# Splat attention and a mixture-of-experts layer: the second half of the heads prepared inside the head loop

## What is computed

```
xn = layernorm(x)
q, k, v = heads of xn @ Wq.T, Wk.T, Wv.T               # 16 heads of 16
feats(z) = exp(-0.5*|z-pos|^2/scale^2), tanh((z-pos).dir)   # 8 splats a head
splat    = (amp*qg) @ kg.T + strength*(amp*qg*qd) @ (kg*kd).T
std = softmax(causal(q k.T/4)) v ; gsa = softmax(causal(q k.T/4 + sens*splat)) v
attn = ((1-blend)*std + blend*gsa) @ Wo.T
idx, w = top 2 of 16 by sqrt(softplus(xn @ gate_w.T)) + gate_b
y = sum of w * expert(xn) over the rows' slots (at most 128 rows an expert)
shared = (silu(xn @ Ws1.T) * (xn @ Ws3.T)) @ Ws2.T
out = x + attn + y + shared
```

## Time and profile before

| | us |
|---|---|
| median of 3 runs | 377.26 (376.95 to 378.29) |
| the profiled execution | 378.75 |
| its span, first to last instruction | 376.9 |

### The profile page before, as it was taken

The page is one execution under the profiler, slowest core; times in us unless marked ns, Lnnn a source line. Parts: engine busy times, 40 slices in busy tenths (PEclk is TensorE's granted clock), DMA queues, the critical chain, the costliest instruction groups (busy, mean ns, idle before and its releaser), DMA issues.

```text
span 376.9 us, 6181 instructions
## 1 busy us (share of the span) xinstructions
PE 334.7 (89%) x2172; PEld 174.8 (46%) x2172; DVE 230.7 (61%) x614; ACT 194.1 (51%) x278; POOL 65.7 (17%) x82
## 2 busy tenths in 40 slices
PE   0999996788979999999999999999999999989965
PEld 0643663343345544554455445544554454335433
DVE  4555857587674665567556655766577558776222
ACT  1699824525414365436543654366346547767530
POOL 7200140400047530110111011102010007710000
PEclk9999768598979999999999999999999999999995
DMA  6408623304341354245655565547555525510011
GB/s 220 131 0 103 107 38 41 60 13 60 47 135 15 41 75 73 71 89 102 142 153 105 113 139 153 107 93 154 129 125 111 79 53 127 143 42 2 0 57 56
DMA packets 27330, 33.01 MB, mean 88 GB/s; under 512 B 6593, under 2 KB 20097, under 8 KB 27297
## 3 DMA queue, kind: packets, MB, share of 16 engines
q1 hardware_dynamic: 23745, 28.32, 37.4%
q0 software_dynamic: 2128, 4.22, 3.9%
q10 hardware_dynamic: 1424, 0.04, 0.2%
HBM read 15.60 MB, written 4.28 MB: 53 GB/s over the span
## 4 chain that ended last, share of the span: by engine, by line
PE 72%; DVE 14%; ACT 9%; issue 3%; DMA 1%; SPq 0%; DVEq 0%; ACTq 0%
PE ps L817 16%; PE ps L745 9%; PE ps L800 8%; PE ps L788 7%; PE ps L754 7%; PE ps L718 6%; ACT arena_p L636 6%; DVE mx L1093 5%; PE ps L676 4%; PE ps L773 2%; PE ps L695 2%; PE ps L758 2%; PE ps L791 2%; DMA acc<-in_x_dram 1%; ACT small L641 1%
## 5 line engine op out<-in xcount | busy, mean ns | idle before, releaser
L636 ACT ACTIVATE arena_p<-ps 128x1024 f32<-128x1024 f32 (+1 forms) x192 | 147.2, 811 | 79.4 <-PE ps L800 53.7
L1093 DVE TENSOR_REDUCE mx<-ps 128x1 f32<-128x512 f32 (+3 forms) x160 | 89.3, 590 | 33.2 <-PE ps L718 22.7
L817 PE MATMUL ps<-arena_p,v_full 128*32 128x512 f32 (+3 forms) x768 | 72.6, 496 | 0.6 <-ACT arena_p L636 0.6
L718 PE MATMUL ps<-stage 96*128 96x512 bf16 (+3 forms) x160 | 51.5, 362 | 7.1 <-DVE mx L1093 4.7
L788 PE MATMUL ps<-stage 98*128 98x512 bf16 (+1 forms) x192 | 51.9, 337 | 4.7 <-ACT arena_p L636 4.2
L800 PE MATMUL ps<-stage 98*128 98x512 bf16 (+1 forms) x192 | 47.4, 332 | 3.0 <-ACT arena_p L636 2.4
L641 ACT ACTIVATE small<-ps 128x176 f32<-128x176 f32 x24 | 7.6, 318 | 64.1 <-PE ps L745 64.1
L387 POOL DMA_INDIRECT wt<-xn_scratch,ids_sb x16 | 15.2, 951 | 133.2 <-PE ps L735 127.6
L817 PEld LDWEIGHTS ps<-arena_p,v_full 128*32 128x32 f32 x768 | 20.2, 110 | 35.4 <-issue 30.3
L754 PE MATMUL ps<-arena_o,small 88*128 88x256 f32 x96 | 27.4, 409 | 8.3 <-DVE small L1116 6.3
L788 PEld LDWEIGHTS ps<-stage 98*128 98x128 bf16 x192 | 18.8, 100 | 23.5 <-ACT arena_p L636 9.8
(11 more groups left out here) (193 smaller groups left out, 418.5 us busy)
## 6 DMA issues: line engine op xcount, KB each, us to landing
w_sb<-in_w_dram SPq DMA_DIRECT2D x16, 352.0 KB
stage<-split SPq DMA_DIRECT2D x48, 96.0 KB, 2.9
stage<-split SPq DMA_DIRECT2D x48, 64.0 KB, 2.7
arena_o<-in_w_dram SPq DMA_DIRECT2D x16, 176.0 KB
stage<-split SPq DMA_DIRECT2D x80, 32.0 KB, 2.5
ye_scratch<-wt SPq DMA_DIRECT2D x16, 128.0 KB, 1.8
stage<-split SPq DMA_DIRECT2D x32, 48.0 KB
acc<-in_x_dram SPq DMA_DIRECT2D x2, 512.0 KB, 4.6
```

The costliest lines, as they stand in the source:

```text
L636: A(to, ps[:, 1 + 2 * s:3 + 2 * s, off:CH], ACT.Exp, scale=SCALE).then_inc(done, 1)
L718: ins = M(b[:, 0:n1 - n0], lhs, ks[0:KR, pr, h, n0:n1], start=True, stop=not diag)
L817: ins = M(ps[c:c + 2 * HD, 0, off:CH], v_full[:, jb + s, g * GH + h, :], of, start=jb + s == 0, stop=end)
L1093: V.reduce_max(mx[:, it // TC, h, it % TC, pc:pc + 1], b[:, 0:n1 - n0], AX.X).then_inc(aux_free, 1)
```

## The change

The heads are prepared in two halves. Before the loop only heads 0 to 7 get projections, features and parts; the second half's are tasks in the table: projections (`proj1`) at slots 26 to 31 counted over all groups (24 a group), features (`feat1`) at 34 to 39, and the parts, rests and thirds at 30 to 53, emptied by ScalarE between the exponentials; the thirds of all parts are VectorE's, and GpSimd has none. q and k features of one half now lie in the two partition halves of one tile, and a group's features are 17 transfers instead of 19. The rows of group 0 are loaded part by part, each as soon as its part is there.

Routing moves to slots 10 to 36, so its first five steps stay in group 0. All of `max1` for group 0 moves into slots 0 to 5 with its shift at 6. The experts run one after the other, every fifth slot from 52 on; the shared expert takes the place of a seventeenth, its eight tiles behind them from slot 133 to 173, and the additions start at 156. In the prologue the gate comes before the features and the values before the first maxima. The parameters arrive in one transfer, and their square root and exponentials come before the evictions.

```diff
-        PRO += [("proj", (s, m, tc)) for m in range(KD) for s in range(2) for tc in range(NC)] + [("par", 0)]
-        PRO += [("feat", (s, tc, w)) for s in range(2) for tc in range(NC) for w in range(2)]
-        PRO += [("gate", 0)] + [("v", n) for n in range(NT // 2)]
+        PRO += [("proj", (s, tc)) for s in range(2) for tc in range(NC)] + [("par", m) for m in range(2)] + [("gate", 0)]
+        PRO += [("feat", (tc, w)) for tc in range(NC) for w in range(2)] + [("v", n) for n in range(NT // 2)]
...
-        LATER = 8
-        first_rest = [(n // 2, ("pre", t)) for n, t in enumerate(max1[LATER:])] + [(4, ("pre", ("shift", 1)))]
-        first_maxima = spread_late(max0, 5, 9) + [(12, ("shift", 0))] + spread_late(max1, 10, 20) + [(22, ("shift", 1))]
+        def chain(kinds, count, at):
+            return [(at + 5 * n + step, (kind, n)) for n in range(count) for kind, step in zip(kinds, (0, 2, 4, 5))]
+        first_rest = [(n // 3, ("pre", t)) for n, t in enumerate(max1)] + [(6, ("pre", ("shift", 1)))]
+        first_maxima = spread_late(max0, 7, 11) + [(13, ("shift", 0))] + spread_late(max1, 11, 21) + [(22, ("shift", 1))]
+        HALF = [(26, ("proj1", (0, 0))), (27, ("proj1", (0, 1))), (30, ("proj1", (1, 0))), (31, ("proj1", (1, 1))),
+                (30, ("p0", 4)), (34, ("p0", 5)),
+                (34, ("feat1", (0, 0))), (35, ("feat1", (0, 1))), (38, ("feat1", (1, 0))), (39, ("feat1", (1, 1))),
+                (41, ("product", 1)), (42, ("p0", 6)), (43, ("p0", 7)),
+                (42, ("rest", 4)), (43, ("rest", 5)), (44, ("p1", 4)), (45, ("p1", 5)), (46, ("third", 4)), (47, ("third", 5)),
+                (48, ("rest", 6)), (49, ("rest", 7)), (50, ("p1", 6)), (51, ("p1", 7)), (52, ("third", 6)), (53, ("third", 7))]
+        S_ROUTE, S_EXPERT, S_SHARED, S_ADD = (10, 36), 52, 133, 156
+        long = HALF + spread([("route", k) for k in range(ROUTE)], *S_ROUTE)
+        long += chain(("xT", "gu", "hT", "y"), E, S_EXPERT)
+        long += [(at, t) for at, t in chain(("-", "sgu", "shT", "sy"), NT, S_SHARED) if t[0] != "-"]
+        long += spread([("add", (k, n)) for n in range(NT) for k in range(2)], S_ADD, 7 * NSLOT + 12)
...
-        PRE1 = max1[0:LATER]
...
+            for j in range(N_F - 1):
+                if ROWS_F[j][0:3] in ((0, 0, 0), (0, 1, 0), (0, 2, 0)):
+                    for at in (2, 3):
+                        wait_parts(sp, at, ROWS_F[j][1])
+                load_feature_row(sp, 0, 0, j, f_in[0])
+            shift_rows(-1, 0, 0)
+            sp.wait_ge(zeros_out, 16)
+            sp.wait_ge(gaps_ready, 1)
+            load_feature_row(sp, 0, 0, N_F - 1, f_in[0])
             for j in range(N_QK):
                 load_qk_row(sp, 1, 1, j, qk_in[1])
...
-                        elif (kind, a) == ("route", ROUTE - 1):
+                        elif (kind, a) == FIRST_WEIGHTS:
                             sp.wait_ge(slots_ready, 2)
-                            for e in range(WB - 1):
+                            sp.wait_ge(aux_full, full_of(("feat1", (1, 1))))
+                            for e in range(WB):
                                 expert_in(e)
...
+                            elif kind in HALVES:
+                                bank, count, _ = place(g, (kind, a))
+                                act.wait_ge(aux_full, count)
+                                if (kind, a) == ("proj1", (0, 0)):
+                                    act.wait_ge(xn_out, 16)
+                                (from_proj if kind == "proj1" else from_feat)(1, *a, ps[:, bank, :], half_free)
+                            elif kind == "p0":
+                                part0(a)
+                            elif kind == "p1":
+                                part1(a)
...
+            rest_of(0)
+            gate()
+            third_of(0)
+            rest_of(1)
+            plus_one()
+            third_of(1)
+            product(0)
             rest_of(2)
             rest_of(3)
-            product(0)
-            rest_of(4)
-            rest_of(5)
-            third_of(4)
-            product(1)
-            rest_of(6)
-            third_of(5)
-            rest_of(7)
+            third_of(2)
+            third_of(3)
```

More of the change, by code:

```diff
@@ L216, in bass_splat_attention_moe_layer @@
         max1 = [("max", (h, it, pc)) for h in range(GH) for it in range(TC, NT) for pc in range(2)]
-        def spread(tasks, first, last):
-            return [(first + (last + 1 - first) * n // len(tasks), t) for n, t in enumerate(tasks)]
         def slotted(*lists):
@@ L272, in bass_splat_attention_moe_layer @@
         PRE0 = max0 + [("shift", 0)]
-        PRE1 = max1[0:LATER]
         AB = 3
-        UNBANKED = ("add", "route")
+        FIRST_WEIGHTS = ("product", 1)
+        OWN_E = next(e for e in range(E) if AT["xT", e] >= OWN_AT[1] * NSLOT)
+        UNBANKED = ("add", "route", "p0", "p1", "rest", "third", "product")
         CUM = 4
-        sequence = [(-1, t) for t in PRE0 + PRE1]
+        sequence = [(-1, t) for t in PRE0]
         for g in range(NG):
@@ L299, in shape_of @@
             return off, jb // TC == ic
-        N_QK, N_F = 12, 19
+        ROWS_QK = [(n, 2 * n + (1 - 2 * n) * step, h) for step in range(3) for n in range(2) for h in range(GH)]
+        ROWS_F = [(n, 2 * n + (1 - 2 * n) * step, h, w) for step in range(3) for n in range(2) for h in range(GH)
+                  for w in ((0, 1) if n == 0 and step < 2 else (None,))]
+        N_QK, N_F = len(ROWS_QK), len(ROWS_F) + 1
         def load_qk_row(eng, g, b, j, done):
-            n, h = j // 6, j % 6 // 3
-            row, part, num = RUNS[j % 3]
+            n, run, h = ROWS_QK[j]
+            row, part, num = RUNS[run]
             head = g * GH + h
@@ L700, in aux @@
                 kind, a = t
[L701 removed]
+                if kind in UNBANKED and t != ("route", CUM):
                     return
[L703 removed]
+                bank, count, _ = place(g, t)
                 b = ps[:, bank, :]
                 if count > AB:
[L706 removed]
+                    pe.wait_ge(*freed[count - 1 - AB])
                 if kind == "max2":
@@ L820, in pv, with own @@
                     ins.then_inc(acc_full, 1)
-            n_v = PRO.index(("v", 0))
-            for n in range(n_v):
-                prologue(n)
-            pe.wait_ge(wide_ready, 1)
-            pe.wait_ge(pro_act, N_ACT)
-            pe.wait_ge(consts, 1)
-            needed = pe.value_load(wide[0:1, 0:1], min_val=0, max_val=1)
-            with pe.If(needed > 0):
-                pe.wait_ge(pro_dve, N_DVE)
-                with pe.Fori(0, NG) as g:
+            def own(half, b, fb):
+                with pe.Fori(half * NG // 2, (half + 1) * NG // 2) as g:
                     pe.wait_ge(own_in, (g + 1) * (16 * (N_QK + N_F - 1)))
@@ L900, in _ @@
                             slot(3)
+                if g + 1 == OWN_AT[1]:
+                    with pe.If(needed > 0):
+                        for n in range(AB):
+                            pe.wait_ge(*freed[DONE_BY[g] - 1 - n])
+                        own(1, g % QB, g % 2)
             pv(NG - 1, NP - 1)
@@ L1064, in route @@
                 elif k == CUM:
-                    bank, count = place(g, ("route", CUM))
-                    dve.wait_ge(aux_full, count)
+                    bank, full, count = place(g, ("route", CUM))
+                    dve.wait_ge(aux_full, full)
                     V.tensor_copy(G[7], ps[:, bank, 0:NT * E].rearrange("p (n e) -> p n e", e=E)).then_inc(aux_free, 1)
@@ L1083, in aux @@
                     return
-                bank, count = place(g, t)
+                if kind in HALVES or kind in ("p0", "p1"):
+                    return
+                if kind in ("rest", "third", "product"):
+                    {"rest": rest_of, "third": third_of, "product": product}[kind](a)
+                    return
+                bank, full, count = place(g, t)
                 b = ps[:, bank, :]
-                dve.wait_ge(aux_full, count)
+                dve.wait_ge(aux_full, full)
                 if kind == "max2":
@@ L1216, in _ @@
                             aux(g, t)
+                if g + 1 == OWN_AT[1]:
+                    with dve.If(needed > 0):
+                        own(1)
             evac(NG - 1, 1)
```

588 lines of the change are left out of this document (278 added, 310 removed).

## The result

The changed kernel takes **392.71 us** (median of 4 runs, 389.52 to 395.27) against 377.77 for the kernel before: a ratio of 1.0385, 95% interval 1.03 to 1.0471. The forecast was 382.5 with a range of 373 to 391, slower at 0.59. The direction was right; the time lies above the range. The profiled execution took 395.27 us, its span is 393.5, and the sum had 382.1.

What follows compares the result with a forecast made beforehand. TensorE bounds the kernel after group 0, so gains come only before 120.65 us. Sum: 97.5 + 186.7 + 46.2 + 21.0 + 12.1 + 0.6 - 1.0 + 7.0 + 12.0 = 382.1 us span; forecast median 382.5, range 373 to 391.

Steps and rivals of the forecast that it cites:

- Start of attention: Prologue to group 0's first third: first score matmul at 52.0 us, second row block's at 71.1, slot 8 at 74.1.
- half clock: Group 0, slots 0 to 7: the stall before slot 7 and sparse TensorE bring half clock, costing the sum nothing extra.
- Rest of group 0: Slots 8 to 23: 23.4 us, from VectorE's 22.7 us of work plus 0.7 for waits.
- the end of group 0 some 23 us earlier: End of group 0: at 97.5 us, where it was 120.65 before.
- routing's last step at slot 30: Routing: last step at about 108 us, scatters and gathers behind it have until slot 52 and cost nothing.
- Projections, features, parts: Second half's tasks in the loop: 12.1 us of TensorE for projections and features, plus 7 us lost to moved parts.
- 7 us for lost cover: Moved parts in slots 26 to 53: 3 us lost through ScalarE and 4 through VectorE, bounds 1 and 11.
- The moved parts are hidden: Rival, chance 0.15: ScalarE's 16 and VectorE's 11 us lie wholly beside TensorE, 7 us go, 375.5 to 377.
- Shared tiles: Behind the experts: 2.63 us a tile, eight 21.0; four in group 0 before partly filled gaps.
- An expert costs 2.89, sixteen 46.2: Groups behind group 0: each expert adds 2.89 us, the old kernel's price, sixteen 46.2; groups 3 and 4 at 40.4.
- SP's waits: SP's queue: waits for slots 39 and 41 hold back five projection rows of group 3; nothing, 2 us if late.
- clock falls in the new gaps: Rival, chance 0.12: three or four gaps of 2 us or more, each followed by 4 us at 1.2 GHz: 389.

Runs made afterwards that it cites:

- y4_shift: Changed kernel with only group 0's second shift sent earlier by SP, at slot 2 ahead of the last eight feature rows: 422.65 us, ratio 1.0262.
- x8: Changed kernel with VectorE's rests and thirds of the second half on 8 columns instead of 1024: 423.4 us, ratio 1.0318 to the kernel before.
- x9: Changed kernel with the second half's rests, thirds and ScalarE's parts 0 and 1 all on 8 columns: 421.36 us, ratio 1.0235 to the kernel before.
- x6: Kernel before without its eight shared tiles and their weights: 392.52 us, ratio 0.9523.
- x4: Kernel before with only its experts put on every fifth slot (steps 0, 2, 4, 5) from slot 48: 416.18 us, ratio 1.0123.
- y2: Changed kernel with experts at six slots each and the kernel before's step distances, SP's rows unchanged (also y2_sixth): 415.89 us, ratio 1.0106.
- x5: Changed kernel with expert and shared chains at steps 0, 2, 5, 7 and SP's projection rows from slot 8 instead of 10: 415.95 us, ratio 1.0101.
- x2: Changed kernel with longer distances in the expert and shared chains (steps 0, 2, 5, 7 instead of 0, 2, 4, 5): 418.4 us, ratio 1.018.
- x7_after_noshared: Changed kernel without its eight shared tiles and their weights: 404.98 us, ratio 0.9826 to the kernel before.
- after_again: Changed kernel unedited, run again on a later chip: 424.57 us, ratio 1.0245 to the kernel before.
- x11: Kernel before with the four value tasks ahead of the first maxima: median 412.66 us against 410.89; three of ten runs at 405 to 408.
- x10: Kernel before with the routing's steps spread over slots 3 to 32 instead of 1 to 22: 409.0 us, ratio 0.9941.

## Why the prediction was right and wrong

**Start of attention: right.** 52.5 for 52.0, second row block 71.08 for 71.1, slot 8 at 75.5 for 74.1. The 71.1 rested on SP's queue alone; but the turned maxima were ready only at 67.1 (65.2 in y4_shift), where the text had VectorE done at 63, so the queue was worth 2 us and less than it was charged, with the same sum. The half clock that the text expected in these slots came for a part of them: the granted clock is 0.72 over the first third.

**Rest of group 0: right in its number, in part by luck.** 23.75 us for 23.4. The largest single forecast, the end of group 0 some 23 us earlier, nearly held (21.4). But VectorE was to set the pace with 22.7 us of work, over 90%, and had 19.49, which is 82%: its closings and steps were charged 3.2 us too high. What fills the stretch is TensorE's 19.68 us and its waits of 4.1: 2.0 for the negated maxima (L947, ahead of the transpose at 96.75), 1.6 in two waits for row maxima to leave their banks (L1131), 0.5 for another VectorE step. The text also has routing's last step at slot 30; the table puts it at 33, which changed nothing.

**Projections, features, parts: right in size.** Groups 1 and 2 took 82.1 us, forecast 81 to 85. Of the 7 us for lost cover, group 2 shows 3.45 (x8, x9), 1.2 of them clock. Group 1 has 41.0 against 26.52 + 12.1 = 38.6, 2.4 more; that this is the parts' too is argued only. "The moved parts are hidden" falls with it.

**Shared tiles: right.** 21.0 forecast, 17 to 20 measured in the new place. What was not seen is that four in group 0 were hardly a bargain there (some 8 of 10.5 us, by the estimate from x6).

**The experts: wrong, and this is the step that failed.** "An expert costs 2.89, sixteen 46.2" took the price of a cadence of six slots, where steps stand 2, 3 and 1 or 2, 2 and 1 slots apart, for one of five slots with 2, 2, 1. Groups 3 and 4 were forecast at 40.4 and took 42.7 and 43.2. Group 5, which the text gave no number, is by the same terms 26.5 + 2.6 experts + 1.8 shared tiles = 38.8, and took 43.8. Groups 6 and 7 have 1.1 more than 39 and about half a us more. This is 11 us together, and 11.4 is what the span has over the sum; 1.8 too few in group 0 stand against 1.1 too many in groups 1 and 2 and 0.65 in the tail. The same cadence in the kernel before costs 5 us (x4), taken back together with the distances it removes the idle time (y2), and lengthened distances with earlier rows give 6 to 9 (x5). In groups 3 and 4, which hold no stall, the runs split it (price 81.4 with the row transposes in group 4): 4.5 us above it in the changed kernel, 2.5 with longer distances (x2), 1.4 with earlier rows too (x5), none with the cadence of six (y2). One us of the first step is the wait at L786 that no edit aimed at and that the trace doesn't explain. Group 5's 5.0 are split by no run, since the stall of the later chips falls there; x7_after_noshared, where it doesn't, has group 5 4.4 us above its price without any shared tile (38.5 for 34.0), so the shared tiles are not its cause.

**SP's waits: wrong.** They were costed at nothing, or 2 us if late, and for the wrong wait. It was not the parts of slots 39 and 41 but the `y` step, at which SP waits before it issues the rows behind: 1.5 us in group 5, followed by half clock (0.54 from 271 to 274 us). Between x2 and x5 lie 2.5 us by the medians and 3.2 by the ratios, which is what the rows are worth, though two runs apart by that are at the edge of their intervals.

The rival "clock falls in the new gaps" (389) named the right kind of loss in the wrong place: group 2 and group 5 have 0.96, which is some 2 us in both together (1.2 in group 2, from y4_shift), and groups 3 and 4 lose their time at a clock of 1.00.

**The balance** on the first chip: 21.4 won in group 0 and about 10.5 in group 1, which lost four shared tiles; spent on the second half's matmuls 12.1, on its parts and group 1's excess 5.9, on eight shared tiles in groups 5 to 7 20, on the experts' closer chains and the late rows about 11: 17 us longer, measured 16.6 in the spans. Even without that loss it stays behind: y2_sixth has a ratio of 1.0106, with stalls about as long as the kernel before has there (some 33 and 34 us), for the change buys a start 12 us earlier with 12 us of TensorE work put into groups in which TensorE has none to spare. Of group 0's gain, some 8 us are the moved tiles, by the estimate above.

## What to carry to other kernels

A price read from an interleaved schedule (so many us for an expert) holds for that schedule's distances: when steps of a dependent chain move closer, charge each link with the engine between them, and look for what else the queue issues behind the chain's last step. Moving work from a prologue into a loop whose bounding engine is at 95% only gains what the prologue idled, so compare those two numbers first. Before moving much, try to thin out the densest small steps beside the first stalls: spreading eight routing steps over eight more slots gained 0.6 to 0.75%, where the whole change lost 2 to 4.

## What was not expected of the hardware

**Stalls around indirect transfers, on some chips.** On the later chips all engines but GpSimd lose 12 to 21 us at each of the same two places, the scatters of ids and the last gathers, in one long gap or in several: in group 1 of after_again TensorE's longest is 4.6 us, VectorE's 6.1 and ScalarE's 10.4. after_again, group 5: TensorE's longest gap, and GpSimd's gathers just ahead of it (timeline).

```profile
341.58 0.48 PE L747 MATMUL ps<-stage 96*128 96x384 bf16 x1 [14.34 <-DVE small L1151]
...
317.10 0.95 POOL L469 DMA_INDIRECT split<-ye_scratch,gidx  x1 [37.62 <-DMA stage<-split]
318.36 0.95 POOL L469 DMA_INDIRECT split<-ye_scratch,gidx  x1 [0.30 <-issue]
```

The VectorE step named had itself waited: VectorE's and ScalarE's own gaps there are 17.4 and 13.5 us, and the trace names nothing of this core as their end. On the first chip the same group has no gap above 1.5 us. The stalls, read as what a group has over its length on the first chip, add 12.4 and 14.6 us in the changed kernel (groups 1 and 5), and in the kernel before 14.8 in groups 0 and 1 (from x11) and 19 to 21 in group 6; they follow the transfers when those are moved (group 6 of y2_sixth, group 1 of x10). What causes them stays open. Since they hit the kernel before harder, the changed kernel's ratio is smaller there.

**The same instructions at another clock.** Slot 8 to the end of group 0, in after_again and in y2_sixth, which has the same tasks there:

```profile
74.39:100.86 26.47, 22.39 (x155) 9.05 (x154) 19.51 (x55) 13.19 (x16) 0.00 (x0) 0.88 0.19 33
...
75.73:99.62 23.89, 19.82 (x155) 8.40 (x154) 19.50 (x56) 13.00 (x16) 0.00 (x0) 0.99 0.19 34
```

VectorE's work and TensorE's waits are equal, and the stretch differs by 2.6 us with the granted clock alone. The Trainium skill ("TensorE: Matmul & The Clock Gate", part 1) says that how many matmuls run slow at a kernel's start varies between runs of one kernel. The two rows show the clock varying in the same way in a later stretch, which the page doesn't speak of. A difference of this size in a stretch that begins after a gap says nothing on an edit.
